# Segment sums of a three-pass graph network: prefix scans, stored sums and a search for each node's last edge give way to one-hot matmuls into node accumulators in SBUF

## The reference, cut to what matters

```python
# pass 0: nodes in blocks of 8 (6,250 "big" nodes of 8 x 16), 5 edge types; indices above 6,249 are
# clamped on the source side and dropped on the destination side
msg = einsum('eoi,eib->eob', W[edge_types - 1], xr[src])
y   = segment_sum(msg, dst, 6250) + segment_sum(Bv[edge_types - 1], dst, 6250)
x   = layernorm(x + y)
# passes 1 and 2: 50,000 nodes, 8 relations
norm = 1 / max(cnt[dst, edge_type], 1)
h    = segment_sum((x[src] @ W[edge_type]) * norm, dst, 50000) + x @ root + bias
# relu after pass 1, log_softmax after pass 2, then layernorm(x1 + h)
```

## Time and profile before

| | us |
|---|---|
| median of 3 runs | 21301.4 (21280.03 to 21308.8) |
| profiled execution, span from first to last instruction | 21305.2 |
| stages: edges / first | 527 / 360 |
| sum of pass 0 | 1646 |
| first layernorm, table of pass 1, rest of the search | 351 |
| pass 1: sum / nodes and table of pass 2 | 8895 / 535 |
| pass 2: sum / nodes, softmax, output | 8452 / 540 |
| POOL busy | 15769.1 |
| DVE / PE busy | 2819.0 / 382.9 |

### The profile page before, as it was taken

The page is one execution under the profiler, slowest core; times in us unless marked ns, Lnnn a source line. Parts: engine busy times, 40 slices in busy tenths (PEclk is TensorE's granted clock), DMA queues, the critical chain, the costliest instruction groups (busy, mean ns, idle before and its releaser), DMA issues. The chain is left out here.

```text
span 21305.2 us, 32941 instructions
## 1 busy us (share of the span) xinstructions
PE 382.9 (2%) x1789; PEld 211.7 (1%) x1790; DVE 2819.0 (13%) x6927; ACT 228.5 (1%) x634; POOL 15769.1 (74%) x15358
## 2 busy tenths in 40 slices
PE   0200110000000000000000100000000000000000
PEld 0100000000000000000000000000000000000000
DVE  0444348000000000000000000000000000000002
ACT  0000000000000000000000100000000000000000
POOL 0588679777777777777777777777777777777777
PEclk9755555555555555555555555555555555555555
DMA  0222210000000000000000210000000000000011
GB/s 39 82 74 68 92 58 6 13 13 13 13 14 13 13 13 13 13 13 14 13 13 13 60 19 13 13 13 13 13 14 13 13 13 13 13 13 13 13 17 21
DMA packets 621296, 487.05 MB, mean 23 GB/s; under 512 B 298800, under 2 KB 549358, under 8 KB 618014
## 3 DMA queue, kind: packets, MB, share of 16 engines
q0 software_dynamic: 491040, 190.45, 7.9%
q1 hardware_dynamic: 125498, 229.95, 3.0%
q10 hardware_dynamic: 4548, 64.87, 0.8%
HBM read 227.17 MB, written 257.09 MB: 23 GB/s over the span
## 5 line engine op out<-in xcount | busy, mean ns | idle before, releaser
L683 POOL DMA_INDIRECT s_rows<-table,s_idx x14116 | 14490.7, 1027 | 4402.9 <-issue 4304.0
L1191 DVE TENSOR_TENSOR s_rows<-s_rows,all_norm 128x1312 f32<-128x1312 f32 x162 | 249.9, 1543 | 15395.5 <-DMA s_rows<-table,s_idx 15395.0
L683 POOL DMA_INDIRECT n_got<-sums,n_idx x784 | 754.6, 963 | 260.5 <-issue 248.0
L1194 DVE TENSOR_TENSOR_SCAN s_rows<-all_keep,s_so_far,s_rows 128x82 f32<-128x82 f32 (+1 forms) x2592 | 743.6, 366 | 20.5
L868 DVE TENSOR_TENSOR_SCAN s_rows<-s_keep,s_rows 128x52 f32<-128x52 f32 x2048 | 339.3, 253 | 848.5 <-DMA s_rows<-table,s_idx 848.5
L683 POOL DMA_INDIRECT x_got<-dst_d,x_idx x224 | 257.5, 1150 | 101.8 <-issue 69.6
L683 POOL DMA_INDIRECT fi_got<-dst_d,early_win_idx x168 | 177.1, 1054 | 156.7 <-DVEq L642 105.8
L886 DVE SCALAR_TENSOR_TENSOR s_rows<-s_carry,s_first,s_rows 128x128 f32<-128x128 f32 x832 | 219.9, 342 | 0.6
L179 POOL TENSOR_SCALAR ed_tmp<-ed_typ 128x6642 int32<-128x6642 int32 x1 | 22.6, 22627 | 256.5 <-DMA ed_typ<-in_edge_type_dram 256.5
L484 POOL IOTA fi_node_i<- 128x392 int32 x1 | 0.6, 618 | 232.6 <-POOLq L89 232.6
L1292 PE MATMUL n1t_turn_ps<-all_ident,n_ends 128*16 128x128 f32 x1 | 0.4, 383 | 8605.4 <-DMA n_ends<-sums 8605.4
(11 more groups left out here) (228 smaller groups left out, 1734.2 us busy)
## 6 DMA issues: line engine op xcount, KB each, us to landing
s_rows<-table,s_idx POOLq DMA_INDIRECT x14116, 2.3
sums<-s_rows SPq DMA_DIRECT2D x162, 656.0 KB, 3.1
sums<-s_rows ACTq DMA_DIRECT2D x16, 3328.0 KB
table<-x1t_out SPq DMA_DIRECT2D x48, 512.0 KB
table<-n1t_out SPq DMA_DIRECT2D x48, 512.0 KB
table<-fi_out SPq DMA_DIRECT2D x48, 320.0 KB
n_got<-sums,n_idx POOLq DMA_INDIRECT x784
sums<-s_zeros ACTq DMA_DIRECT2D x8, 832.0 KB, 8.5
```

What stands on the lines that cost most here:

```text
L683: pool.indirect_dma_start(out=out[:, j, :], out_offset=None, in_=table, in_offset=bass.IndirectOffsetOnAxis(ap=idx[:, j:j + 1], axis=0)).t ...
L1191: st(nc.vector.tensor_tensor(rows[:, b, :, :], rows[:, b, :, :], scale, ALU.mult))
L1194: one = nc.vector.tensor_tensor_scan(rows[:, b, :, f], env.keep[:, bass.ds(w * WIN, WIN)], rows[:, b, :, f], so_far[:, f:f + 1], ALU.mult, ...
```

## The change: what it does

The edge list now lies as tiles of 128 consecutive edges, one edge on each partition: column t of an index tile is tile t (6,656 tiles with padding). Destinations are grouped by 128 nodes ("groups of nodes", 391 of them, 49 in pass 0). A list of **steps** is made on the chip: step s multiplies tile t(s) into group w(s), with s = t + w; where a tile holds edges of two groups, it is used twice. There are 7,040 steps (for 6,656 tiles and 391 groups). For each step DVE makes a 128 x 128 matrix that is 1 where the edge's destination is the node (`hot`, eight steps in one instruction, L1025 of the new kernel; its first input lies in PSUM), and PE multiplies it with the tile's gathered rows into a PSUM bank that holds eight groups of nodes; where it reads and writes there comes out of registers that a load from SBUF fills (L980). After eight steps DVE adds the bank's 8 x 16 (in pass 0: 8 x 128) columns to the accumulators in SBUF at a place from a register (L1015 to L1019). Two banks and two `hot` buffers alternate.

Since tile t is used at step t + w(t), the last 384 of the 7,040 steps come after the last tile's block: 6 blocks of 64 steps behind the block that waits for the last gather.

Gone are: the scans, the stores of running sums, the carries, the search and its 392 gathers, and the 49 + 784 gathers that read sums back, with the patches between partitions. New are 64 gathers (110 partitions, 512 bytes each) that bring the destinations of each step, turns of the index and `norm` lists on PE and ACT (from one list per partition to one edge per partition), tables of steps that go through HBM to one partition, and lists loaded as 112, 15 and 1 rows. `Norm` keeps its two scans per relation, has one maximum scan in place of a scan and a product, and a predicated copy in place of a product and a sum; its sums over first and last runs become 16 tensor-scalar instructions with one input. `Table` has its copies split between ACT and DVE. The root term and x1 are loaded by node with pieces of 64 bytes during the gathers of passes 1 and 2; the output leaves with pieces of 64 bytes.

```diff
-def load(eng, to, frm, landed):
-    eng.dma_start(to[0:rows, :], frm[0:split].rearrange("(p c) -> p c", p=rows)).then_inc(landed, 16)
+LIST_PARTS = ((0, 112), (112, 127))
+def load_list(eng, to, frm, landed):
+    for a, z in LIST_PARTS:
+        eng.dma_start(to[a:z, :], frm[a * COLS:z * COLS].rearrange("(p c) -> p c", c=COLS)).then_inc(landed, 16)
...
 # stage_edges, PE: the bias of pass 0 by a matmul, mul_ps is one buffer
+for k, (a, z) in enumerate(((0, 512), (512, width))):
+    nc.tensor.matmul(mul_ps[:, k, 0:z - a], x_turned[:, t % 2, :], mix[:, a:z], start=True, stop=False)
+    last = nc.tensor.matmul(mul_ps[:, k, 0:z - a], one_row[:, :], bias_row[:, a:z], start=False, stop=True)
...
 # stage_sum0: ring of 4 blocks of 32 gathers; the same steps with 128 columns
-for f in range(ROW0):
-    one = nc.vector.tensor_tensor_scan(rows[:, b, :, f], keep[:, :], rows[:, b, :, f], 0.0, ALU.mult, ALU.add)
+for c in range(2):
+    nc.tensor.matmul(ps[g % 2][:, c * 512:(c + 1) * 512], zero[:, 0:P], zero[:, :], start=True, stop=False, ...)
+for j, v in enumerate(where):
+    last = nc.tensor.matmul(ps[g % 2][:, bass.ds((v % GROUP) * ROW0, ROW0)], hot[:, g % 2, j, :],
+                            rows[:, bass.ds(v // GROUP, 1), :]..., start=False, stop=True, ...)
...
 # Norm.dve, for each relation
-stl(nc.vector.tensor_tensor(count[:, :], count[:, :], self.is_end[:, :], ALU.mult))
+st(nc.vector.tensor_tensor_scan(count[:, ::-1], self.keep[:, COLS:0:-1], count[:, ::-1],
+                                self.start[:, 1, r:r + 1], ALU.mult, ALU.max))
+st(nc.vector.copy_predicated(self.norm[:, :], self.mine.bitcast(U16), count[:, :]))
...
+def stage_layer(nc, env, name, table, bias, first_layer):        # in place of stage_sum1
+    # POOL: RING = 13 blocks of SPAN = 64 gathers
+    with pool.Fori(0, TURNS) as i:
+        for b in range(RING):
+            pool.wait_ge(idx_in[b], (i + 1) * 16)
+            pool.wait_ge(free, i * RING + b + 1)
+            fetch(pool, rows[:, b * SPAN:(b + 1) * SPAN], table, idx[:, b], SPAN, landed[b])
+    # PE
+    def span(m):
+        for g in range(per):                                      # per = 8 groups of GROUP = 8 steps
+            _, where = nc.values_load_multi_w_load_instructions(
+                env.steps[0:1, bass.ds(m * SPAN + g * GROUP, GROUP)], engines=[pe.engine], ...)
+            pe.wait_ge(hot_ready, m * per + g + 1)
+            pe.wait_ge(added, m * per + g + 1)
+            nc.tensor.matmul(sums[g % 2], zero[:, :], zero[:, :], start=True, stop=False, ...)
+            for j, v in enumerate(where):
+                last = nc.tensor.matmul(sums[g % 2][:, bass.ds((v % GROUP) * FEAT, FEAT)], hot[:, g % 2, j, :],
+                                        rows[:, bass.ds(v // GROUP, 1), :]..., start=False, stop=True, ...)
+            last.then_inc(multiplied, 1)
+    with pe.Fori(0, HOLD) as m:                                   # HOLD = 8
+        pe.wait_ge(scaled, m + 1); span(m)
+    with pe.Fori(HOLD, TURNS * RING) as m:
+        pe.wait_ge(scaled, m + 1); span(m); pe.sem_inc(free, 1)
+    with pe.Fori(TURNS * RING, SPANS) as m:                       # 104 .. 109: no gathers behind them
+        span(m)
+    # DVE, each block: scale (one input in PSUM), then its eight groups
+    nc.vector.tensor_copy(scale_ps, env.big0[:, bass.ds(m * SPAN, SPAN)]).then_inc(scale_ready, 1)
+    dve.wait_ge(landed[b], (i + 1) * (16 * SPAN))
+    nc.vector.tensor_tensor(at, at, scale_ps..., ALU.mult).then_inc(scaled, 1)
+    nc.vector.tensor_tensor(hot[:, g % 2, :, :], lane_ps..., local..., ALU.is_equal).then_inc(hot_ready, 1)
+    nc.vector.tensor_tensor(at, at, sums[g % 2]..., ALU.add).then_inc(added, 1)
...
-def stage_nodes1(nc, env, name, sums, root_d, bias, x1_d, table_args):
+def stage_middle(nc, env, weights, table):                        # Table alone, from the accumulators
+def stage_output(nc, env):                                        # softmax and layernorm, 7 chunks of 56 groups
```

More of the change, by code:

```diff
@@ L135, in _ @@
+        idx0_ready, idx1_ready, wide_turned, wide_read, idx_out = map(s.sem, (
+            "idx0_ready", "idx1_ready", "wide_turned", "wide_read", "idx_out"))
+        stored = [s.sem(f"stored{b}") for b in range(2)]
+        block = s.block()
+        table0 = env.table0.rearrange("(n r) f -> n (r f)", n=NODES0)
+        batches = PER // 4
+        half, part = SPAN // 2, SPAN // PARTS
         @block.sync
         def _(sp):
-            sp.wait_ge(padded, 3)
-            load(sp, typ, env.dst, dst_in)
@@ L185, in _ @@
+            act.wait_ge(idx1_ready, 1)
+            turned_lists(typ8, batches)
         @block.tensor
         def _(pe):
[L187 to L190, removed]
+            pe.wait_ge(small_in, 16 * (CH + 2))
+            pe.wait_ge(below_ready, 1)
+            nc.tensor.matmul(bend_ps[:, 0:WINS], ones[:, :], below[:, :], start=True, stop=True
+                             ).then_inc(bend_ready, 1)
@@ L938, in stage_x1 @@
+        tb = Table(nc, env, s, x_sb, weights, table, env.root1_d, None, False)
         block = s.block()
@@ L1140, in stage_sum1 @@
-        norm = Norm(nc, env, s) if with_norm else None
-        block = s.block()
-        out = sums.rearrange("(p c) f -> p c f", p=P)
-        turns = WINS // RING
-        @block.gpsimd
-        def _(pool):
-            with pool.Fori(0, turns) as i:
-                for b in range(RING):
-                    pool.wait_ge(idx_ready, i * RING + b + 1)
-                    pool.sem_inc(claimed, 1)
-                    fetch(pool, rows[:, b], table, idx[:, b], WIN, landed[b])
-        @block.sync
@@ L1242, in stage_nodes1 @@
+        idx_in = [s.sem(f"idx_in{b}") for b in range(RING)]
+        landed = [s.sem(f"landed{b}") for b in range(RING)]
+        norm = Norm(nc, env, s, ps) if first_layer else None
+        sums = [ps[:, b * 512:b * 512 + GROUP * FEAT] for b in range(2)]
+        lane_ps = ps[:, 2 * 512:2 * 512 + P]
+        scale_ps = ps[:, 3 * 512:3 * 512 + SPAN]
+        acc, root = env.acc, env.root
+        per = SPAN // GROUP
+        by_node = lambda d: d.rearrange("(w n) f -> n w f", n=P)
         block = s.block()
@@ L1298, in _ @@
+def stage_middle(nc, env, weights, table):
+    with ExitStack() as ctx:
+        s = Scope(nc, ctx, "mid")
+        values = env.acc[:, 0:CH * WINS0, :].rearrange("n (t o) f -> n t (o f)", o=CH)
+        root = env.root.rearrange("n (t o) f -> n t (o f)", o=CH)
+        tb = Table(nc, env, s, values, weights, table, None, root, True)
+        block = s.block()
+        @block.sync
+        def _(sp):
+            tb.load_weights(sp)
+            tb.sp(sp)
         @block.scalar
         def _(act):
-            if tb:
-                tb.act(act)
```

1799 lines of the change are left out of this document (794 added, 1005 removed).

## The result

The changed kernel takes 19952.6 us (median of four runs, 19949.6 to 19956.6) against 21296.2 us for the kernel before, measured beside it: a ratio of 0.937, 95% interval 0.9354 to 0.938. It is faster by 1344 us; the time is 223 us above the 19730 that were forecast.

What follows compares the result with a forecast made beforehand. POOL's pace, 1.25 us per gather, was taken as the bound. Edges 380, pass 0 1200, first layernorm 200, pass 1 8975, nodes 150, pass 2 8690 and output 130 sum to 19725, rounded to 19730; range 19150 to 20600.

Steps and rivals of the forecast that it cites:

- Edges: First stage, edges and first tables: 887 to 380 us, with lists loaded in three parts and 49 tiles at 3.4.
- if the tiles start under the loads: Lower bound of the first stage, edges and first tables: 300 us against 380 forecast.
- The bound of 600: Upper bound of the first stage: 600 us if tiles run at half clock and lists come at half the rate.
- the rival of the dear stages: Bare stages cost more: edges 600, pass 0 1350, output and root 100 more; 20230 us in all; 15%.
- A group of eight steps: PE's work per group in passes 1 and 2: 6.0 us, hidden during gathers, bare for 56 groups behind the last.
- the +72: Pass 1: forecast 8975 us from gathers, a head loss of 284 and a tail of 346; measured 9047.
- the +55: Pass 2: forecast 8690 us as 8320 of gathers, 346 of tail and 25; measured 8745.
- The bound of 10.2: Upper bound in us of a group in passes 1 and 2: slow array passes, registers and eight loads at 0.303.
- The head of pass 1: Start of pass 1: `Norm` and other list-long DVE work holds POOL for 334 us, losing 284 us of gathers.
- about 250: Sign to look for in the changed profile: about 250 gathers in the first 550 us of pass 1.
- PE sets the pace: Passes 1 and 2: groups pass the 9.45 us that gathers allow; at 11 us a group the total is 21985; 9%.
- PE is quick: Tails of passes 1 and 2: a group takes 3 us, so they are 336 us shorter, total 19390; 17%.

Runs made afterwards that it cites:

- e_lane_sbuf: Changed kernel, passes 1 and 2: the one-hot comparison reads lane numbers from SBUF instead of PSUM, so both inputs lie in SBUF; 20818.2 us.
- e_hot_twice: Changed kernel, passes 1 and 2: VectorE makes each one-hot group twice, lane numbers still from PSUM; 19951.7 us.
- e_bias_rows: Changed kernel with the first stage's bias matmul given 128 rows (bias in row 0, zeros below) instead of one; 19807.5 us.
- e_list_127: Changed kernel with each edge list loaded as one piece of 127 rows instead of 112 and 15; 20328.5 us.
- e_no_load: Changed kernel, passes 1 and 2: a group's eight values are not read, each step uses the next tile and a fixed column; 19624.9 us.
- e_narrow: Changed kernel, passes 1 and 2: only the first 32 of 128 nodes of each window are summed, register work stays; 19952.2 us.
- e_load_twice: Changed kernel, passes 1 and 2: each group's eight values are read and range-checked twice; 23982.0 us.
- e_no_bias: Changed kernel without the bias matmul of the first layer's table, product tile still single-buffered; 19813.7 us.

## Why the prediction was right, and where it was off

- **What bounds the kernel** was right: POOL's pace of 1.25 us, undisturbed by `hot` with its first input in PSUM. e_lane_sbuf and e_hot_twice show it from both sides.
- **Edges, +151 us.** Three terms were wrong, and one of them hid part of the others. The tiles begin at 54 us and not at 140 (-86): the bound "if the tiles start under the loads" is what happened. A tile was priced at 3.4 us from the earlier trace rows, rows at the faster pace, and takes 6.73 (e_bias_rows, with the same passes at the faster pace, is 145 us shorter): 334 us, with one wait of 5 for x, instead of 170 (+164). Behind the tiles 143 us pass, where 60 and "a little waiting" (10) were taken (+73), since three of the four parts of the 64 gathers do not lie "beside the tiles". That these sum to 151 is partly luck. The bound of 600 "if they run at half clock" named one cause; it stood in the rival of the dear stages, with 15%. The loading of the lists in parts was right, and worth more than it was priced at: e_list_127 takes 376 us more without it.
- **A group of eight steps, 6.0 forecast, 7.35 measured.** The sum put 4.2 of array and 1.9 of registers in series, 6.1, and took 6.0. They are not in series: the array (4.25, e_no_load) lies under a queue of 7.3. The array's term was right and did not count (e_narrow); the registers' term was too small by a factor of nearly four, because eight values load in 1.921 us and not in 0.303, and because 34 register operations were priced at 0.046 us each where the median is 0.146 in the load's check and 0.100 at the steps. Fifty-six groups of 1.35 are 75 us per pass: that is the +72, and with other small terms the +55. The bound of 10.2 held.
- **The Trainium skill's 200 ns per register** (Runtime: NRT & Kernel Launch, Instruction fetch mechanics) gave 7.3 us for a group and 146 us more for the sum. That page speaks of register loads from HBM; the trace comes near its figure for these loads from SBUF: 1.921 / 8 = 0.24 us per value. It deserved more weight, since the one row against it was a load of one value. That it came out at 7.3 is partly luck: it prices neither the checks nor the overlap.
- **The head of pass 1**: 284 forecast, 297 measured. The scans and predicated copies hold gathers: 24 end in the 300 us of the eight relations. The 16 instructions with one input that replace the products do not: 7.1 us each, with gathers going out beside them at 0.8 per us. One input is not enough to leave gathers alone, though. List-long comparisons without a sum (L848, 3.6 us each, half the time for as many elements) hold a gather too:

```profile
1949.34 7.28 DVE L848 TENSOR_SCALAR all_big<-all_big,l1n_start 128x6656 bf16<-128x6656 int32 x2
```

```profile
1953.44 3.99 POOL L108 DMA_INDIRECT l_rows<-table,l_idx  x1 [0.30 <-issue]
```

  The forecast counted them as holding, and its sum gives 213 gathers in the first 550 us (550 / 1.25 less 227), near the 209 in 558; the "about 250" under its signs does not follow from that sum.
- **Rivals.** "PE sets the pace" was real: a group would have to grow by 2.1 us to pass 9.45, and e_load_twice shows what comes then; its price per group was right and its fixed part per block was missing. "PE is quick" fell: even without the load and its check a group takes 4.25 us, not 3. "The bare stages are dear" was half right, in the first stage only; its parts, 220 + 150 + 100, give 20200 and not 20230. Of a price of pieces of 64 bytes nothing shows (output 107 us, forecast 130), but no run tried them by themselves.

## What to carry to other kernels

Price an engine's queue and its array apart and take the longer, not the sum: here a load of eight register values cost nearly eight prices, and the range checks (2.25 us) more than the load (1.92). Ask of every DVE instruction beside indirect gathers how many of its inputs lie in SBUF, and look for one such meeting in a trace before trusting the answer. Where a stage is bare, read the duration of one known matmul in it before pricing columns. When work is said to lie beside other work, check in the code what its buffer waits for: 93 us of gathers did not.

## What the runs showed of the hardware that I had not expected

- With a bias matmul of one row (`1*128`) in each tile TensorE stays slow: the transposition is 0.48 us, and 0.33 with a bias matmul of 128 rows and the same columns. Making the operand larger made the kernel 145 us shorter.
- The granted clock that the profile records does not tell this. Of the changed kernel and of e_no_bias it says 1.00, which would be 2.4 GHz, in stretches where the transposition takes 0.48 and 0.47 us (busy us of PE, PEld, DVE, ACT, POOL, then the clock):

```profile
200.00:300.00 100.00, 84.52 (x133) 32.03 (x133) 0.00 (x0) 16.68 (x60) 0.00 (x0) 1.00 0.13 49
```

```profile
130.00:200.00 70.00, 50.58 (x95) 25.54 (x95) 4.80 (x2) 20.95 (x76) 14.49 (x12) 1.00 0.27 99
```

  In e_list_127 the same tiles with the same durations (0.48) stand beside a record of 0.50, which would be 1.2 GHz:

```profile
450.00:700.00 250.00, 211.50 (x336) 80.38 (x335) 0.00 (x0) 41.37 (x148) 0.00 (x0) 0.50 0.13 49
```

  The Trainium skill (TensorE: Matmul & The Clock Gate, Seeing it yourself) calls such records unreliable on trn2; here the durations decide.
- A short DVE instruction with two SBUF inputs costs POOL's gathers two fifths of its length on the mean (0.49 of 1.22 us), since one that starts right behind a gather costs nothing.
- Three lists loaded as 127 rows and one keep the SyncE queue busy with issuing for 324 us, and as 112, 15 and one rows for 4 us; every transfer that it issues behind them starts later by that (e_list_127).
